# A graph layer's last stage: normalisation product on ScalarE, residual sum on GpSimd, stores on SyncE

## The reference

```python
moe = jnp.sum(topk_w[..., None] * sel, axis=2)   # two experts per node
y = x + moe                                      # x: layer-normed input of this part
mu = jnp.mean(y, axis=-1, keepdims=True)
var = jnp.var(y, axis=-1, keepdims=True)
return (y - mu) / jnp.sqrt(var + EPS) * gamma + beta
# and around it: out = residual + (the value above)
```

## Time and profile before

| what | value |
|---|---|
| median of three runs | 3244.35 us (3242.36 to 3245.18) |
| profiled execution, span from first to last instruction | 3251.7 us |
| profiled execution, a time beside its span | none is recorded |
| busy over the span: TensorE, VectorE, GpSimd, ScalarE | 2607.0, 2245.8, 2005.7, 1343.0 us |
| instructions | 53650 |
| first diagonal and last store issue of the last stage | 3159.9 and 3247.5 us |

### The profile page before, as it was taken

The page is one execution under the profiler, slowest core; times in us unless marked ns, Lnnn a source line. Parts: engine busy times, 40 slices in busy tenths (PEclk is TensorE's granted clock), DMA queues, the critical chain, the costliest instruction groups (busy, mean ns, idle before and its releaser), DMA issues. The chain is left out here.

```text
span 3251.7 us, 53650 instructions
## 1 busy us (share of the span) xinstructions
PE 2607.0 (80%) x12447; PEld 1725.7 (53%) x12447; DVE 2245.8 (69%) x5185; ACT 1343.0 (41%) x3219; POOL 2005.7 (62%) x2128
## 2 busy tenths in 40 slices
PE   4999968797878879887888978788763509999987
PEld 2555534444545454554545445454442508888875
DVE  7888867787878777777777878787769804222228
ACT  1444445454545545454455545455431102222223
POOL 1666657777777777777777777777773752222220
PEclk9999988899989898899989989999985559999999
DMA  5111125545454544544445554544440247777756
GB/s 152 38 36 37 38 63 145 141 141 147 136 148 136 148 142 140 141 141 141 142 141 148 142 142 142 141 141 142 141 140 13 100 147 232 233 234 233 232 181 203
DMA packets 305265, 453.73 MB, mean 140 GB/s; under 512 B 117079, under 2 KB 206148, under 8 KB 305017
## 3 DMA queue, kind: packets, MB, share of 16 engines
q0 software_dynamic: 87024, 243.45, 26.5%
q1 hardware_dynamic: 187469, 135.23, 14.5%
q10 hardware_dynamic: 30540, 72.47, 6.7%
HBM read 395.75 MB, written 56.83 MB: 139 GB/s over the span
## 5 line engine op out<-in xcount | busy, mean ns | idle before, releaser
L944 POOL DMA_INDIRECT rows_g<-node_rows,idx x1568 | 1490.6, 951 | 493.1 <-issue 450.2
L1161 PE MATMUL p_m<-msg,sel 128*128 128x264 f32 x3520 | 1020.5, 439 | 275.1 <-DVE msg L1129 192.3
L1161 PEld LDWEIGHTS p_m<-msg,sel 128*128 128x128 f32 x3520 | 712.3, 213 | 410.2 <-issue 288.4
L1129 DVE TENSOR_TENSOR msg<-rows_g,p_w 128x1024 f32<-128x1024 f32 x440 | 535.0, 1216 | 15.7 <-ACT p_w L1034 12.8
L1034 ACT ACTIVATE p_w<-lg 128x32 f32<-128x32 f32 x440 | 88.5, 201 | 799.7 <-DVE lg L1122 799.3
L1741 POOL DMA_INDIRECT moe<-ysb,token x128 | 123.5, 965 | 377.2 <-DVE ysb L1729 355.8
L1001 ACT ACTIVATE sel_t<-apart,ones 128x512 bf16<-128x512 bf16 x443 | 319.8, 722 | 32.1 <-issue 2.1
L1059 DVE TENSOR_TENSOR sel<-p_w,dst_t 128x512 f32<-128x512 f32 x441 | 304.1, 690 | 25.4 <-issue 7.5
L998 ACT ACTIVATE apart<-dst_all,iota_neg 128x512 bf16<-128x512 bf16 x443 | 313.3, 707 | 8.9 <-DMA dst_all<-dst_bc 8.9
L1118 DVE TENSOR_TENSOR lg<-rows_g,ends 128x32 f32<-128x32 f32 x440 | 85.5, 194 | 327.1 <-SPq L965 220.2
L1697 ACT ACTIVATE ht<-e_ph,ba 128x256 f32<-128x256 f32 x256 | 100.5, 475 | 451.2 <-PE e_ph L1667 451.2
(11 more groups left out here) (317 smaller groups left out, 3416.7 us busy)
## 6 DMA issues: line engine op xcount, KB each, us to landing
dst_all<-dst_bc ACTq DMA_DIRECT2D x112, 512.0 KB
wa<-in_L_ffn_w_dram SPq DMA_DIRECT2D x64, 512.0 KB, 3.6
wb<-in_L_ffn_w_dram SPq DMA_DIRECT2D x64, 512.0 KB, 4.8
rows_g<-node_rows,idx POOLq DMA_INDIRECT x1568
xs<-slot_x SPq DMA_DIRECT2D x64, 258.0 KB, 3.9
ya<-moe SPq DMA_DIRECT2D x48, 256.0 KB, 3.5
bb<-in_L_ffn_b_dram SPq DMA_DIRECT2D x64, 128.0 KB, 5.3
qs<-qn_dram ACTq DMA_DIRECT2D x14, 512.0 KB
```

Source lines behind the costliest of these rows:

```text
L944: pool.indirect_dma_start(rows_g[:, j, u, :], None, node_rows, bass.IndirectOffsetOnAxis(ap=idx[q][:, j, u:u + 1], axis=0)).then_inc(gathe ...
L1129: dve.tensor_tensor(m4, g3[:, :, 0:D].rearrange("p u (h e) -> p u h e", h=H), p_w[:, 0:TC * H].rearrange("p (u h) -> p u h", u=TC).unsquee ...
L1161: mm = pe.matmul(p_m[j % 2][:, 0:ROW], sel[j][:, u, :], msg[j % 2][:, u, :], start=(u == 0), stop=(u == TC - 1))
```

## The change

ScalarE no longer issues stores. In each round it takes the square root of group i first, then builds the diagonals of group i+2, then multiplies the two tiles of group i-1 by the reciprocal deviation (new function `spread`: an activation Copy with a scale operand, in place in `xl`). VectorE's step begins with the statistics of the new group; the reciprocal of the old one comes behind them, and the subtraction and product with gamma (two instructions, unchanged in form) take the place of the fused product and sum. GpSimd adds the residual, one instruction for a group of two full tiles (`ready` now counts groups). SyncE issues the stores behind the loads of later groups. TensorE waits for `centred` where it waited for `sums_used`; both are signalled behind the same instruction.

```diff
@@ scalar
+                def spread(i):
+                    act.wait_ge(centred, i + 1)
+                    for t in groups[i]:
+                        o = act.activation(xl[0:rows(t), t, :], xl[0:rows(t), t, :], ACT.Copy, scale=rs[0:rows(t), t:t + 1])
+                    o.then_inc(normed, 1)
+
                 for i in range(2):
                     weights(i)
                 for i, g in enumerate(groups):
+                    act.wait_ge(var_ready, i + 1)
+                    act.sqrt(rs[:, g[0]:g[-1] + 1], rs[:, g[0]:g[-1] + 1]).then_inc(std_ready, 1)
                     if i + 2 < len(groups):
                         weights(i + 2)
-                    act.wait_ge(var_ready, i + 1)
-                    act.sqrt(rs[:, g[0]:g[-1] + 1], rs[:, g[0]:g[-1] + 1]).then_inc(std_ready, 1)
                     if i:
-                        store(groups[i - 1])
-                store(groups[-1])
-                act.wait_ge(stored, BLOCKS * 16)
+                        spread(i - 1)
+                spread(len(groups) - 1)
@@ vector
-                    if old:
-                        dve.wait_ge(std_ready, i)
-                        dve.reciprocal(rs[:, old[0]:old[-1] + 1], rs[:, old[0]:old[-1] + 1])
-                        for a, t in enumerate(old):
-                            n = rows(t)
-                            o = dve.scalar_tensor_tensor(out=xl[0:n, t, :], in0=p_sum[(i - 1) % SUMS][0:n, a * D:(a + 1) * D], scalar=ag[0:n, t, 0:1],
-                                                         in1=g_b[0:n], op0=ALU.subtract, op1=ALU.mult)
-                        o.then_inc(sums_used, 1)
                     if new:
                         dve.wait_ge(rows_summed, new[-1] + 1)
                         for a, t in enumerate(new):
                             dve.bn_stats(st[0:rows(t), t, :], p_sum[i % SUMS][0:rows(t), a * D:(a + 1) * D])
+                    if old:
+                        dve.wait_ge(std_ready, i)
+                        dve.reciprocal(rs[:, old[0]:old[-1] + 1], rs[:, old[0]:old[-1] + 1])
                     dve.drain()
                     for t in new:
                         dve.bn_aggr(ag[0:rows(t), t, :], st[0:rows(t), t, :])
-                    for t in old:
+                    for a, t in enumerate(old):
                         n = rows(t)
-                        dve.scalar_tensor_tensor(out=xl[0:n, t, :], in0=xl[0:n, t, :], scalar=rs[0:n, t:t + 1], in1=resid[0:n, t, :],
-                                                 op0=ALU.mult, op1=ALU.add).then_inc(ready, 1)
+                        o = dve.scalar_tensor_tensor(out=xl[0:n, t, :], in0=p_sum[(i - 1) % SUMS][0:n, a * D:(a + 1) * D], scalar=ag[0:n, t, 0:1],
+                                                     in1=g_b[0:n], op0=ALU.subtract, op1=ALU.mult)
+                    if old:
+                        o.then_inc(centred, 1)
@@ gpsimd (new)
+                for i, g in enumerate(groups):
+                    pool.wait_ge(normed, i + 1)
+                    if len(g) == 2 and rows(g[1]) == P:
+                        q = xl[:, g[0]:g[1] + 1, :]
+                        pool.tensor_tensor(q, q, resid[:, g[0]:g[1] + 1, :], ALU.add).then_inc(ready, 1)
+                    else:
...
@@ tensor
-                    wait(pe, sums_used, i - SUMS + 1)
+                    wait(pe, centred, i - SUMS + 1)
@@ sync
+                def store(i):
+                    sp.wait_ge(ready, i + 1)
+                    for t in groups[i]:
+                        sp.dma_start(out[t * P:t * P + rows(t), :], xl[0:rows(t), t, :]).then_inc(stored, 16)
+
+                for t in range(YR):
+                    fetch(t)
+                for i, g in enumerate(groups):
+                    for t in g:
+                        if t + YR < BLOCKS:
+                            fetch(t + YR)
+                    if i >= 2:
+                        store(i - 2)
...
```

More of the change, by code:

```diff
@@ L1761, in gps_layer @@
             rows_summed = sem("rows_summed", c)
-            sums_used = sem("sums_used", c)
+            centred = sem("centred", c)
+            normed = sem("normed", c)
             var_ready = sem("f_var_ready", c)
@@ L1775, in _ @@
             def _(act):
[L1776 to L1779, removed]
                 def weights(i):
@@ L1833, in _ @@
                 step(len(groups), [], groups[-1])
+            @block.gpsimd
+            def _(pool):
+                for i, g in enumerate(groups):
[5 more added lines that the diff above has]
+                        for t in g:
+                            n = rows(t)
+                            o = pool.tensor_tensor(xl[0:n, t, :], xl[0:n, t, :], resid[0:n, t, :], ALU.add)
+                        o.then_inc(ready, 1)
             @block.tensor
@@ L1850, in _, with fetch @@
             def _(sp):
-                for t in range(BLOCKS):
+                def fetch(t):
                     wait(sp, rows_summed, t - YR + 1)
                     sp.dma_start(ya[t % YR][0:rows(t)], moe[0:2 * NP, :].rearrange("(k r) f -> r k f", k=2)[t * P:t * P + rows(t)]).then_inc(y_in[t % YR], 16)
+                def store(i):
[5 more added lines that the diff above has]
+                for i, g in enumerate(groups):
+                    for t in g:
+                        if t + YR < BLOCKS:
+                            fetch(t + YR)
+                    if i >= 2:
+                        store(i - 2)
+                for i in range(len(groups) - 2, len(groups)):
+                    store(i)
+                sp.wait_ge(stored, BLOCKS * 16)
         late.close()
```

## The result

The changed kernel takes 3254.68 us (median of 9 runs, 3250.74 to 3257.95), the kernel before, in runs beside it, 3245.18 us (9 runs, 3241.78 to 3249.40). The ratio is 1.0028, 95% interval 1.0020 to 1.0036: slower by 6.5 to 11.7 us.

What follows compares the result with a forecast made beforehand. VectorE was taken to bound the last stage at 3.24 us a group; the 6.64 us loop over two groups plus the hold gave 3.61, and with the tail +9.4 us: 3253.7 us, range 3245 to 3258, a little more above, 3260.

Steps and rivals of the forecast that it cites:

- VectorE's 3.24 us: Last stage before the change: VectorE, without a gap but the variance, sqrt, reciprocal trip, sets 3.24 us per two-tile group.
- TensorE's 2.60 us: Last stage: TensorE alone could do a group of two tiles in 2.60 us.
- The closed loop: Last stage: late diagonals make TensorE and VectorE wait for each other over two groups, 6.64 us, or 3.32 a group.
- The hold: VectorE's variance instruction is held until the GpSimd add ends, making the period 3.61 us a group; forecast's chance 0.66.
- rival B: VectorE's L1813 is held by the GpSimd add too: 4.25 us a group, 14 us more, 3267.8 us; chance 0.06.
- The sum: Whole kernel: groups at 3.61 us plus the tail end the span 9.4 us later; added to the median, 3253.7 us.
- S(23): Start of the sqrt of group 23 in the last stage, forecast at 3251.4 us, with 9.7 us to the end.
- A (no hold): Variance instruction slips in beside the GpSimd add: two groups take 6.64 us, +3.0 us, 3247.4 us; chance 0.18.
- C: TensorE's pace decides, 2.60 us a group, needing a loop under 5.2 us: -12.8 us, 3231.6 us; chance 0.07.
- D: TensorE idles more and its clock slows: 4.22 us a group, 13 us more, 3267 us; chance 0.03.
- SyncE: SyncE issuing the stores delays loads 1.3 us; cost taken as zero, no gain, upper end 0.9 us a group.

Runs made afterwards that it cites:

- e3: Changed kernel with the diagonals of group i+2 built before the wait for the variance of group i; stage 79.1 us, ratio 0.9957 to the kernel before.
- e5: Kernel before with only the sqrt of group i moved ahead of the diagonals of group i+2; stage 91.8 us, ratio 0.9996 to the kernel before.
- e2: Changed kernel without the GpSimd residual add, its semaphore still passed on; stage 91.5 us, ratio 0.9995 to the kernel before.
- e1: Changed kernel with the two-element variance instruction L1827 split into instructions of one element each; stage 95.5 us, ratio 1.0013 to the kernel before.
- e8: Changed kernel without L1827, epsilon added as bias in ScalarE's sqrt; stage 83.1 us, ratio 0.9958 to the kernel before.
- e10: Changed kernel with the stores issued by ScalarE again instead of SyncE; stage 99.8 us, ratio 1.0009 to the kernel before.
- e4: Changed kernel with a second GpSimd add of the same size, into a scratch tile, before each add; stage 98.9 us, ratio 1.0019 to the kernel before.
- e6: Changed kernel with one memset of about 1 us on VectorE in group 1 only; stage 100.0 us, ratio 1.0021 to the kernel before.
- e7: The changed kernel again, unedited, on another chip; stage 100.2 us, ratio 1.0035 to the kernel before.

## Why the prediction was right

**What bounded the kernel before.** VectorE's 3.24 us. Taking L1825 and the sqrt's trip from it (e3) let TensorE's 2.60 us through; the loop by itself gives 3.27 with the old step (e5) and 3.29 with the new one (e2), a second ceiling of nearly the same height.

**The closed loop.** Predicted 6.64 us for two groups, measured 6.59 without the hold (e2) and 6.63 in e1 (sqrts at 4078.90 and 4085.53). Right, and its cause shown by e3.

**The hold.** Predicted from three rows of other stages; in 21 groups L1827 is longer than by itself and ends 0.02 to 0.03 us behind the add. Shown by e1 and e2. Predicted 3.61 us a group, measured 3.58. Two errors cancelled: the add took 1.27 us and not 1.15, but it began 2.25 us behind the sqrt and not 2.37, mostly because GpSimd starts 0.08 us behind the Copies, not 0.16. What is left is L1827's end behind the add, 0.03 and not 0.05, and 0.01 of rounding. The rule behind it was drawn too wide: the prediction has every one-source SBUF-to-SBUF instruction held, and the reciprocal is one that is not (e8). That it stayed harmless here is luck: in the changed kernel the reciprocal does not meet an add in the steady part.

**L1813 beside the add** (rival B): L1821, the same instruction, took 451 to 483 ns after, and in each steady period the add starts in the middle of its pair. Right to leave it free.

**The sum.** Predicted +9.4 us, the stage shows +7.3, the medians +9.5 with an interval of 6.5 to 11.7. Within the stage: 21 of the 22 distances were 0.04 us shorter each (-0.8 us); the last of them was only 3.01 us, since the last group has two diagonals and so the Copies and the add before it came early and L1827 was no longer held (0.17 us), which I had not followed (-0.6); the tail behind S(23) took 9.3 us and not 9.7; the first two groups were 0.35 us quicker. That the median's shift came closer to my number than the stage's own does not make the sum better than it was.

**The rivals.** A (no hold) would have been e1, which keeps the add: its stage is 3.7 us above that of before, and A had 3.0. C needed the loop below 5.2 us; e3 shows what it was worth, at 2.59 us a group. D: the granted clock was 1.00 in every ten microseconds from 3165 to 3235 us, with TensorE busy 7.8 to 8.3 of each ten. SyncE: no effect (e10).

**What I got wrong meanwhile.** Not in the prediction but behind it: e4 (the hold taken as a sum over groups) and e6 (a phase taken as stable without looking at TensorE's own rate).

## What to carry to other kernels

When work is taken off the bounding engine, write down the loop in which the others wait for each other: here one reordered line closed a loop of 6.6 us over two groups, which cost next to nothing with the old step (e5) and 20 us of 99 after (e3). Before GpSimd gets arithmetic next to VectorE, list VectorE's small tensor_scalar and cast instructions on the path and look in a trace which of them are held; a small size does not protect them (two elements 740 ns, one element 153; a reciprocal of two elements 148), and the cheapest mend may be to fold them into another engine's instruction (e8). A price that depends on two engines meeting can't be scaled with the length of either: look for the distances at which the schedule settles.

## What the runs showed of the hardware that I had not expected

- A tensor_scalar of two elements per partition is held beside a GpSimd add, the same on one element is not (153 ns, e1), and a reciprocal of two elements is not (148 ns, e8).
- Between two adds that follow each other at once a held tensor_scalar can slip in, 0.02 to 0.03 us behind the first (e4, groups 2 to 5).
- A GpSimd add of 128x512 took 1038 ns with the same tensor as both inputs into a fresh tile (e4), 1147 in L520, and 1268 in place with two different inputs (L1839 of the changed kernel).
- An occupation by GpSimd of 2.3 us in place of 1.27 made the period shorter, 3.37 against 3.49 us (e4, e7), by moving the meetings. The two ran on different chips, and their stages, 98.9 and 100.2 us, differ by little more than the uncertainty; the distances of the sqrts in the steady part, 6.8 to 6.9 us for two groups against 7.16, do not leave it in doubt.
